# Attention slots handled two at a time: scores of two pairs in one group on TensorE, their 128x128 parts written to the transposition banks

## The chip, the cores and the metric

The kernel runs on one core of one Trainium2 chip. The metric is the device time of one execution in microseconds (us), lower is better. Engines are named as in the profile: PE is TensorE's matmul stream, PEld its weight loads, DVE VectorE, ACT ScalarE, POOL GpSimd, SP the engine that issues most of the DMAs.

## The reference, cut to what matters

```python
x = L0_attn_x                                   # (8, 256, 128)
xn = _layernorm(x)
# attention, 16 heads of 64, latent 64
q = einsum('bsd,qd->bsq', x, wq); kv = einsum('bsd,ld->bsl', x, w_kv_down)
k, v = einsum('bsl,ql->bsq', kv, w_k_up), einsum('bsl,ql->bsq', kv, w_v_up)
q, k = rope(q), rope(k)
probs = softmax(q @ k.T / sqrt(64) + causal)    # per head, 256 x 256
s = (probs @ v) @ wo.T
# eight experts of 128 -> 512 -> 128, one of them per token
g = silu(2 * expert_of_token(xn))
return x + s * g
```

## The kernel before

The attention runs over 64 pairs of heads (8 batches times 8 pairs); pair g belongs to batch g // 8. There is one slot for each pair, g = 0 to 63. The experts' part stands between slots 39 and 40 (`G_LEAD` = 40). Each engine has its own `slot(g)`, written by hand, and `program` calls it in order; the engines meet through semaphores alone, so each engine's order is exactly the order of the code.

A pair's way through the engines: PE projects q and k of two pairs in two **items** (`project(m)`, an even item is q, an odd one k), DVE multiplies them by the rotation (`rotate`, L585), POOL adds the two halves (`rotated`, L463) and SP moves them into `qk_sb` (`place`, L363). Six to eight slots later PE makes the **scores** of pair g + 2 in slot g (`scores`, L1080 the rows 128 to 255 against 256 keys, L1082 the **corner**, rows 0 to 127 against 128 keys), each for the two heads side by side in 64 rows of the array, into `s_bank[0]` and `s_bank[1]`. DVE masks them and takes the row maximum (`row_max`, L594, a corner and a rest for each head), ACT takes the exponential with the sum (`exponentials`, L885), DVE the reciprocal (`denominators`, L601), and DVE, ACT and POOL scale (`scale`: L612, L898, L474; in slots with a scatter or gather POOL scales only the 256-wide parts). PE transposes the probabilities of pair g (`turn`, L1092, three 128x128 blocks for each head, into `t_bank[0]` and `t_bank[1]`), ACT copies them to `probsT` (`turned_probs`, L907), PE multiplies with the latents (`values`, L1106 and L1108, for two pairs at once from slot 24 on), ACT copies the result (`ctx_out`, L914), and PE adds the pair's part of the batch's output into `y_bank` (`output`, L1120).

POOL also issues one indirect DMA in each of the slots 22 to 37 (`scatter`, L482: tokens sorted by expert) and 43 to 58 (`gather`, L490: the experts' results back). At the slots in `FINALS` DVE finishes a batch (`finalise`, L769 to L775) and SP stores it.

`TWICE` names the slots in which one more item is handled; before them items run 6 slots ahead, after the first 7, after the second 8. The last item, 63, falls in slot 55, so from slot 56 on there is nothing to project, rotate or stage. `ALONE` names the pairs whose values are taken singly.

The order of PE in an even slot g from 24 on: scores of g + 2, the item, `turn(g)`, an output, the values of g - 2 and g - 1. In an odd one: scores, item, turn, an output.

## Time and profile before

| what | us |
|---|---|
| median of 3 runs (310.02 to 311.63) | 310.27 |
| the profiled execution | 311.37 |
| its span, first to last instruction | 309.6 |
| PE busy | 296.1 (96%) |
| PEld busy | 237.5 (77%) |
| ACT busy | 242.8 (78%) |
| DVE busy | 221.1 (71%) |
| POOL busy | 215.8 (70%) |

The span is 1.8 us shorter than the profiled execution's own time; the median of the runs lies 1.1 us under that execution. Busy shares are averages over stages with different limits. Matmuls overlap in the records, so PE's share says little about waiting; its pace is read from the starts of successive groups. Times in the rows are from the start of the span.

### The profile page before, as it was taken

How to read it: one execution, taken by the hardware profiler on the slowest of the kernel's cores; microseconds unless marked ns; L12 is line 12 of the kernel's file. 1: busy time of each engine (PE TensorE's matmuls, PEld its weight loads, DVE VectorE, ACT ScalarE, POOL GpSimd, SP SyncE). 2: the span in 40 equal slices, each digit the busy share in tenths (PEclk: the TensorE clock that was granted, in tenths of full speed). 3: DMA queues.
4: the chain of work that ended last, by engine and by line, in shares of the span. 5: the costliest groups of instructions: out<-in, count | busy, mean ns of one | idle time of the engine just before them, and what ended most of it. 6: DMA issues, size and time to landing. Idle time of an engine off the chain costs nothing.

```text
span 309.6 us, 8479 instructions
## 1 busy us (share of the span) xinstructions
PE 296.1 (96%) x2358; PEld 237.5 (77%) x2358; DVE 221.1 (71%) x883; ACT 242.8 (78%) x851; POOL 215.8 (70%) x321
## 2 busy tenths in 40 slices
PE   8889999999999999999999989999989999899994
PEld 3578788888888888777777789999867777786763
DVE  4879998987787998988888523232268789898651
ACT  3376889898877789989897665555699999889982
POOL 3367978687777779999999943322138999889730
PEclk9987999999999999999999999999999999999998
DMA  6754595869433333333345470000063334344200
GB/s 207 231 135 112 96 263 151 216 168 298 113 69 71 65 73 86 95 87 87 88 101 138 124 210 0 2 2 0 3 186 71 89 103 112 105 109 131 74 18 18
DMA packets 39597, 33.35 MB, mean 108 GB/s; under 512 B 4802, under 2 KB 36675, under 8 KB 39555
## 3 DMA queue, kind: packets, MB, share of 16 engines
q1 hardware_dynamic: 38098, 30.51, 38.5%
q0 software_dynamic: 1024, 2.10, 2.5%
q8 instruction: 20, 0.33, 0.5%
q10 hardware_dynamic: 432, 0.23, 0.3%
q14 instruction: 23, 0.18, 0.2%
HBM read 11.07 MB, written 4.98 MB: 52 GB/s over the span
## 4 chain that ended last, share of the span: by engine, by line
PE 65%; POOL 12%; issue 11%; DVE 8%; ACT 2%; DMA 1%; POOLq 1%; SPq 0%; DVEq 0%; ACTq 0%
PE bank L1092 9%; PE bank L1080 9%; PE bank L1106 7%; PE bank L1120 6%; PE bank L1299 6%; PE bank L1284 6%; POOL probs L474 5%; POOL staged L463 4%; PE bank L1054 4%; PE bank L1082 3%; DVE rot_out L585 3%; PE bank L1108 3%; DVE masked L594 2%; PE bank L1070 2%; PE bank L1056 2%
## 5 line engine op out<-in xcount | busy, mean ns | idle before, releaser
L885 ACT ACTIVATE pexp<-masked,negmax 128x128 f32<-128x128 f32 (+1 forms) x256 | 114.1, 452 | 1.7 <-DVE negmax L594 1.6
L474 POOL TENSOR_SCALAR probs<-pexp,rden 128x256 f32<-128x256 f32 (+1 forms) x184 | 80.3, 451 | 27.0 <-DVE rden L601 24.2
L594 DVE CUSTOM_DVE_ANT_0 masked<-bank,mask 128x128 f32<-128x128 f32 (+1 forms) x256 | 75.9, 352 | 28.0 <-PE bank L1082 27.8
L463 POOL TENSOR_TENSOR staged<-rot_out 128x512 f32<-128x512 f32 x63 | 80.2, 1274 | 17.7 <-DVE rot_out L585 17.2
L585 DVE TENSOR_TENSOR rot_out<-bank,rot 128x1024 f32<-128x1024 f32 x64 | 77.7, 1215 | 4.0 <-PE bank L1056 2.7
L907 ACT COPY probsT<-bank 128x384 f32<-128x384 f32 x128 | 55.0, 480 | 23.8 <-PE bank L1092 23.2
L1092 PE MATMUL bank<-ident,probs 128*128 128x128 f32 x384 | 55.3, 278 | 1.8 <-ACT probsT L907 0.9
L885 ACT ACTIVATION_READ_ACCUMULATOR pexp<-masked,negmax 128x1 f32 x256 | 49.8, 195 | 0.0
L1080 PE MATMUL bank<-qk_sb 64*128 64x256 f32 x256 | 45.7, 434 | 2.6 <-DVE negmax L594 1.9
L1092 PEld LDWEIGHTS bank<-ident,probs 128*128 128x128 f32 x384 | 43.7, 141 | 5.0 <-POOL probs L474 1.8
L1120 PE MATMUL bank<-vo_sb,ctxT 128*128 128x128 f32 x256 | 39.5, 279 | 0.7 <-ACT ctxT L914 0.7
L1038 ACT ACTIVATE probsT<-bank,w_own 128x128 f32<-128x128 f32 x88 | 25.1, 368 | 18.8 <-PE bank L1284 18.8
L1106 PE MATMUL bank<-probsT,lat_all 128*64 128x256 f32 (+1 forms) x184 | 37.7, 488 | 0.3 <-ACT probsT L907 0.3
L1120 PEld LDWEIGHTS bank<-vo_sb,ctxT 128*128 128x128 f32 x256 | 33.7, 191 | 1.9 <-ACT ctxT L914 1.1
L549 POOL COPY w_own<-w_sb 128x516 f32 x22 | 13.5, 616 | 27.4 <-ACT probsT L1038 27.4
L1080 PEld LDWEIGHTS bank<-qk_sb 64*128 64x128 f32 x256 | 19.9, 188 | 16.2 <-issue 13.7
L1082 PEld LDWEIGHTS bank<-qk_sb 64*128 64x128 f32 x256 | 25.5, 190 | 2.7
L914 ACT COPY ctxT<-bank 128x256 f32<-128x256 f32 (+1 forms) x46 | 20.7, 451 | 6.8 <-PE bank L1108 5.6
L1082 PE MATMUL bank<-qk_sb 64*128 64x128 f32 x256 | 25.5, 275 | 0.0
L1299 PE MATMUL bank<-w_sb,probsT 128*128 x176 | 24.4, 282 | 0.7 <-issue 0.4
L1108 PEld LDWEIGHTS bank<-probsT,lat_all 128*64 128x64 f32 x184 | 13.3, 137 | 14.3 <-issue 10.3
L1284 PE MATMUL bank<-probsT,w_own 128*128 128x128 f32 x176 | 23.4, 277 | 0.7 <-DVE probsT L854 0.4
(113 smaller groups left out, 459.8 us busy)
## 6 DMA issues: line engine op xcount, KB each, us to landing
qk_sb<-staged SPq DMA_DIRECT2D x128, 128.0 KB, 2.6
w_sb<-in_w SPq DMA_DIRECT2D x2, 1024.0 KB, 5.8
w_sb<-in_w SPq DMA_DIRECT2D x4, 512.0 KB, 4.9
sorted_x<-z SPq DMA_DIRECT2D x1, 1408.0 KB, 7.9
sorted_g<-z SPq DMA_DIRECT2D x1, 1152.0 KB, 5.6
out<-res SPq DMA_DIRECT2D x8, 128.0 KB, 1.9
x_sb<-in_x SPq DMA_DIRECT2D x3, 256.0 KB, 3.2
rot<-in_c_rot SPq DMA_DIRECT2D x1, 512.0 KB, 5.6
```

The costliest lines, as they stand in the source:

```text
L463: pool.tensor_tensor(staged[:, n % 2, :, m % 2, :], rot_out[:, m % 2, :, 0:S], rot_out[:, m % 2, :, S:2 * S], op=ALU.add).then_inc(staged_ ...
L474: pool.tensor_scalar(probs[:, g % 2, i, c], pexp[:, g % 2, i, c], rden[:, g % 2, i, k:k + 1], 1.0, ALU.mult, ALU.mult).then_inc(probs_read ...
L585: dve.tensor_tensor(rot_out[:, m % 2], bank_of(m)[:].unsqueeze(1).broadcast_to([P, 2, 2 * S]), rot[:], op=ALU.mult).then_inc(rope_done, 1)
L594: t = dve.tensor_tensor_reduce(masked[:, g % 2, i, c], s_bank[i][:, c], mask[:, c], -1.0, -NEG * 1e8, ALU.add, ALU.min, negmax[:, g % 2, i ...
L885: e = act.activation(pexp[:, g % 2, i, c], masked[:, g % 2, i, c], ACT.Exp, bias=negmax[:, g % 2, i, k:k + 1], scale=-1.0, accum_out=rowsu ...
L907: act.copy(probsT[:, g % 4, i, :], t_bank[i][:, 0:SW]).then_inc(probsT_ready, 1)
L1080: pe.matmul(s_bank[i][:, P:SW], qk_sb[r, 0, p, P:S], qk_sb[r, 1, p, :], start=True, stop=True)
L1082: m = pe.matmul(s_bank[i][:, 0:P], qk_sb[r, 0, p, 0:P], qk_sb[r, 1, p, 0:P], start=True, stop=True)
L1092: t = pe.transpose(t_bank[i][:, k * P:(k + 1) * P], probs[:, g % 2, i, k * P:(k + 1) * P], ident[:])
L1106: pe.matmul(o[r, :, :], lat_all[:, 2 * b, :], probsT[:, pairs, i, 0:S], start=True, stop=False)
L1120: m = pe.matmul(y_bank[:, i * C:(i + 1) * C], ctxT[:, p, i * P:(i + 1) * P], vo_sb[:, p, :], start=(p == 0 and i == 0), stop=(p == NP - 1) ...
L1299: m = pe.matmul(bank[6 + i][:, 0:C], hidT[:, i, k, :], w2_sb[:, k, :, :].rearrange("p e c -> p (e c)")[:, bass.ds(e * C, C)], start=(k == ...
```

## The change

The slots 24 to 37 and 40 to 61 (`coupled`) are handled two at a time by a new `couple(g)` on each engine, g even. Slots 0 to 23, 38, 39, 62 and 63 keep `slot(g)`.

- PE: `scores_of_two(g + 2)` makes the rests of two pairs into the two halves of `s_bank`, then the two pairs' corners into columns 0 to 255 of `t_bank`. The corners wait until ACT has copied the transposes of pair g - 1 out of that bank. Then come both items, `turn(g)`, the outputs of g - 4 and g - 3, `turn(g + 1)`, and the values of g - 2 and g - 1. `turn` waits for a new semaphore, `corner_read`: DVE must have read both corners.
- DVE: `row_max` becomes `corner_max` (both pairs' corners at once, at the couple's start) and `rest_max`; around them the denominators, scales, rotations and finals of the two slots.
- ACT: within a couple the copies of turned probabilities, the exponentials of pairs g + 2 and g + 3 and, last, `ctx_out(g - 2)`; it used to stand between the two halves of an exponential.
- POOL and SP: the old order of the two slots. `TWICE` goes from (36, 38) to (23, 38), so items run 7 ahead from slot 24 instead of 36.
- Outputs come a couple later; slots 38 and 62 hold one more `output` each, of pairs 34 and 58.

```diff
...
-TWICE = (36, 38)
+TWICE = (23, 38)
...
+def coupled(g):
+    return FIRST_DOUBLE <= g < G_LEAD - 2 or G_LEAD <= g < B * NP - 2
+def corners_through(g):
+    return sum(1 for n in range(g + 1) if coupled(n - 2))
...
-        def program(start, slot, finish, experts):
+        def program(start, slot, couple, finish, experts):
...
-                slot(g)
+                if not coupled(g):
+                    slot(g)
+                elif g % 2 == 0:
+                    couple(g)
...
-                if g + 1 < B * NP and g != G_LEAD:
+                if g + 1 < B * NP:
...
+            def couple(g):
+                for n in range(g, g + 2):
+                    if n != G_LEAD:
+                        scale(n + 1)
+                    for m in items(n):
+                        rotated(m)
+                    if SCATTER_SLOT <= n < SCATTER_SLOT + NT:
+                        scatter(n - SCATTER_SLOT)
+                    if GATHER_SLOT <= n < GATHER_SLOT + NT:
+                        gather(GATHER_ORDER[n - GATHER_SLOT])
...
+            def corner_max(g):
+                dve.wait_ge(scores_done, g + 1)
+                wait(dve, exp_done, 2 * g - 2)
+                for i in range(2):
+                    t = dve.tensor_tensor_reduce(masked[:, g % 2, i, 0:P], t_bank[i][:, g % 2 * P:(g % 2 + 1) * P], mask[:, 0:P],
+                                                 -1.0, -NEG * 1e8, ALU.add, ALU.min, negmax[:, g % 2, i, 0:1])
+                t.then_inc(corner_read, 1)
+            def rest_max(g):
+                for i in range(2):
+                    dve.tensor_tensor_reduce(masked[:, g % 2, i, P:SW], s_bank[i][:, g % 2 * S:(g % 2 + 1) * S], mask[:, P:SW],
+                                             -1.0, -NEG * 1e8, ALU.add, ALU.min,
+                                             negmax[:, g % 2, i, 1:2]).then_inc(masked_ready, 1)
...
-                if 0 < g // NP < LEAD and g % NP == (2 if NP * (g // NP) <= FIRST_DOUBLE else 3):
+                if 0 < g // NP < LEAD and g % NP == (2 if NP * (g // NP) < FIRST_DOUBLE else 3):
...
-                if g + 1 < B * NP and g != G_LEAD:
+                if g + 1 < B * NP:
...
+            def couple(g):
+                corner_max(g + 2)
+                corner_max(g + 3)
+                if g != G_LEAD:
+                    denominators(g + 1)
+                    scale(g + 1)
+                rest_max(g + 2)
+                for m in items(g):
+                    rotate(m)
+                if (g + 1) // NP < LEAD and (g + 1) % NP == 3:
+                    take_y((g + 1) // NP - 1)
+                if FINALS.get(g + 1, -1) >= LEAD:
+                    finalise(FINALS[g + 1])
+                rest_max(g + 3)
+                denominators(g + 2)
+                scale(g + 2)
+                for n in range(g, g + 2):
+                    if FINALS.get(n, LEAD) < LEAD:
+                        finalise(FINALS[n])
+                for m in items(g + 1):
+                    rotate(m)
...
-                more = g + 1 < B * NP and g != G_LEAD
+                more = g + 1 < B * NP and not coupled(g - 1)
...
-                if g > 1 and g - 2 in ALONE and g not in (G_LEAD, G_LEAD + 1):
+                if g > 1 and g - 2 in ALONE:
...
-                if g % 2 and g > 2 and g - 3 not in ALONE and g not in (G_LEAD + 1, B * NP - 1):
+                if g % 2 and g > 2 and g - 3 not in ALONE and g != B * NP - 1:
...
-                if more:
+                if g + 1 < B * NP:
...
+            def couple(g):
+                if g == FIRST_DOUBLE:
+                    exponentials(g + 1, 0)
+                    ctx_out(g - 2)
+                    exponentials(g + 1, 1)
+                if g != G_LEAD:
+                    scale(g + 1)
+                turned_probs(g)
+                for i in range(2):
+                    exponentials(g + 2, i)
+                turned_probs(g + 1)
+                scale(g + 2)
+                for i in range(2):
+                    exponentials(g + 3, i)
+                if g == FIRST_DOUBLE:
+                    ctx_out(g - 1)
+                elif g != G_LEAD:
+                    ctx_out(g - 2)
...
+            def scores_of_two(g):
+                pe.wait_ge(masked_ready, 2 * g)
+                for n in range(2):
+                    p = (g + n) % NP
+                    pe.wait_ge(qk_in[p], 32 * (g // NP) + 32)
+                    for i, r in enumerate(half_rows):
+                        pe.matmul(s_bank[i][:, n * S:(n + 1) * S], qk_sb[r, 0, p, P:S], qk_sb[r, 1, p, :], start=True, stop=True)
+                pe.wait_ge(probsT_ready, 2 * (g - 2))
+                for n in range(2):
+                    p = (g + n) % NP
+                    for i, r in enumerate(half_rows):
+                        m = pe.matmul(t_bank[i][:, n * P:(n + 1) * P], qk_sb[r, 0, p, 0:P], qk_sb[r, 1, p, 0:P],
+                                      start=True, stop=True)
+                m.then_inc(scores_done, 2)
...
+                wait(pe, corner_read, corners_through(g + 3 - g % 2))
...
-                if g > 2 and g - 3 not in ALONE and g not in (G_LEAD, G_LEAD + 1, G_LEAD + 2):
+                if g in (G_LEAD - 2, B * NP - 2):
+                    output(g - 4)
+                if g > 2 and g - 3 not in ALONE:
...
-                if g > 1 and g - 2 in ALONE and g not in (G_LEAD, G_LEAD + 1):
+                if g > 1 and g - 2 in ALONE:
...
-                if g > 0 and g - 1 in ALONE and g != G_LEAD:
+                if g > 0 and g - 1 in ALONE:
...
-                if g > 1 and g % 2 == 0 and g - 2 not in ALONE and g != G_LEAD:
+                if g > 1 and g % 2 == 0 and g - 2 not in ALONE:
...
+            def couple(g):
+                scores_of_two(g + 2)
+                for m in (*items(g), *items(g + 1)):
+                    project(m)
+                turn(g)
+                if g == FIRST_DOUBLE:
+                    output(g - 2)
+                elif g == FIRST_DOUBLE + 2:
+                    output(g - 3)
+                elif g not in (G_LEAD, G_LEAD + 2):
+                    output(g - 4)
+                    output(g - 3)
+                turn(g + 1)
+                if g == FIRST_DOUBLE:
+                    values(g - 1)
+                elif g != G_LEAD:
+                    values(g - 2)
...
```

Left out are the line that makes `corner_read`, the calls that pass `couple`, and SP's `couple`, which calls `slot` twice.

PE in the second half, from the output ahead of the scores of pair 54 to the first matmul of the next item, in the kernel before (bank0 and bank1 are `s_bank`, bank2 and bank3 `t_bank`, bank7 `y_bank`, bank6 the values'):

```order
L1120 MATMUL bank7<-vo_sb,ctxT 128x128 [waits ctx_ready,y_read]
L1120 MATMUL bank7<-vo_sb,ctxT 128x128
L1080 MATMUL bank0<-qk_sb 128x256 [waits masked_ready,qk_in6]
L1080 MATMUL bank1<-qk_sb 128x256
L1082 MATMUL bank0<-qk_sb 128x128
L1082 MATMUL bank1<-qk_sb 128x128
L1054 MATMUL bank4<-xnT_h,wq_h 128x256 [waits rope_done]
L1055 MATMUL bank4<-xnT_l,wq_h 128x256
L1056 MATMUL bank4<-xnT_h,wq_l 128x256
L1054 MATMUL bank4<-xnT_h,wq_h 128x256
```

The same place in the changed kernel, here for pairs 62 and 63, the last group, from the values ahead of it to the transposes of pair 60:

```order
L1209 MATMUL bank6<-probsT,lat_all 64x512 [waits probsT_ready,ctx_ready]
L1209 MATMUL bank6<-probsT,lat_all 64x512
L1211 MATMUL bank6<-probsT,lat_all 64x2x128 x2
L1178 MATMUL bank0<-qk_sb 128x256 [waits qk_in6,masked_ready]
L1178 MATMUL bank1<-qk_sb 128x256
L1178 MATMUL bank0<-qk_sb 128x256 [waits qk_in7]
L1178 MATMUL bank1<-qk_sb 128x256
L1183 MATMUL bank2<-qk_sb 128x128 [waits probsT_ready]
L1183 MATMUL bank3<-qk_sb 128x128
L1183 MATMUL bank2<-qk_sb 128x128
L1183 MATMUL bank3<-qk_sb 128x128
L1195 MATMUL bank2<-ident,probs 128x128 [waits probs_ready00,probsT_ready,corner_read]
```

Two pairs' scores stand together, their corners in bank2 and bank3 and behind a wait for `probsT_ready`; the first transpose waits for `corner_read` too. In couples 24 to 54 two items stand between the corners and that transpose, in 56, 58 and 60 nothing.

PE in slot 62 before, from the outputs of pairs 58 (slot 61) and 59 to the first transpose of pair 62:

```order
L1120 MATMUL bank7<-vo_sb,ctxT 128x128 [waits ctx_ready]
L1120 MATMUL bank7<-vo_sb,ctxT 128x128
L1120 MATMUL bank7<-vo_sb,ctxT 128x128 [waits ctx_ready]
L1120 MATMUL bank7<-vo_sb,ctxT 128x128
L1106 MATMUL bank6<-probsT,lat_all 64x512 [waits probsT_ready,ctx_ready]
L1106 MATMUL bank6<-probsT,lat_all 64x512
L1108 MATMUL bank6<-probsT,lat_all 64x2x128 x2
L1092 MATMUL bank2<-ident,probs 128x128 [waits probs_ready00,probsT_ready]
```

and in the changed kernel, from the values of pairs 58 and 59, the end of couple 60, to the first transpose of pair 62:

```order
L1209 MATMUL bank6<-probsT,lat_all 64x512 [waits probsT_ready,ctx_ready]
L1209 MATMUL bank6<-probsT,lat_all 64x512
L1211 MATMUL bank6<-probsT,lat_all 64x2x128 x2
L1223 MATMUL bank7<-vo_sb,ctxT 128x128 [waits ctx_ready]
L1223 MATMUL bank7<-vo_sb,ctxT 128x128
L1223 MATMUL bank7<-vo_sb,ctxT 128x128 [waits ctx_ready]
L1223 MATMUL bank7<-vo_sb,ctxT 128x128
L1209 MATMUL bank6<-probsT,lat_all 64x512 [waits probsT_ready,ctx_ready]
L1209 MATMUL bank6<-probsT,lat_all 64x512
L1211 MATMUL bank6<-probsT,lat_all 64x2x128 x2
L1195 MATMUL bank2<-ident,probs 128x128 [waits probs_ready00,probsT_ready,corner_read]
```

Before, the values of 58 and 59 stood a slot further ahead of output 58, with scores and a turn between; now they stand directly before it.

ACT at the same place before, from the exponentials of pair 62 to the copy of the values of pairs 60 and 61 (L914 the second time):

```order
L885 ACTIVATE pexp,rowsum<-masked,negmax 128x128 [waits probs_ready00,masked_ready]
L885 ACTIVATE pexp,rowsum<-masked,negmax 128x256 [waits probs_ready01]
L914 COPY ctxT<-bank6 128x512 [waits y_step,pv_done]
L885 ACTIVATE pexp,rowsum<-masked,negmax 128x128 [waits probs_ready10,masked_ready]
L885 ACTIVATE pexp,rowsum<-masked,negmax 128x256 [waits probs_ready11]
L907 COPY probsT<-bank2 128x384 [waits probsT_done,pv_done]
L907 COPY probsT<-bank3 128x384 [waits probsT_done]
L885 ACTIVATE pexp,rowsum<-masked,negmax 128x128 [waits probs_ready00,masked_ready]
L885 ACTIVATE pexp,rowsum<-masked,negmax 128x256 [waits probs_ready01]
L885 ACTIVATE pexp,rowsum<-masked,negmax 128x128 [waits probs_ready10,masked_ready]
L885 ACTIVATE pexp,rowsum<-masked,negmax 128x256 [waits probs_ready11]
L914 COPY ctxT<-bank6 128x512 [waits y_step,pv_done]
```

and in the changed kernel, again from the exponentials of pair 62 on:

```order
L952 ACTIVATE pexp,rowsum<-masked,negmax 128x128 [waits probs_ready00,masked_ready]
L952 ACTIVATE pexp,rowsum<-masked,negmax 128x256 [waits probs_ready01]
L952 ACTIVATE pexp,rowsum<-masked,negmax 128x128 [waits probs_ready10,masked_ready]
L952 ACTIVATE pexp,rowsum<-masked,negmax 128x256 [waits probs_ready11]
L974 COPY probsT<-bank2 128x384 [waits probsT_done,pv_done]
L974 COPY probsT<-bank3 128x384 [waits probsT_done]
L952 ACTIVATE pexp,rowsum<-masked,negmax 128x128 [waits probs_ready00,masked_ready]
L952 ACTIVATE pexp,rowsum<-masked,negmax 128x256 [waits probs_ready01]
L952 ACTIVATE pexp,rowsum<-masked,negmax 128x128 [waits probs_ready10,masked_ready]
L952 ACTIVATE pexp,rowsum<-masked,negmax 128x256 [waits probs_ready11]
L981 COPY ctxT<-bank6 128x512 [waits y_step,pv_done] x2
```

The copy of the values of pairs 58 and 59 stood in the middle of the exponentials of pair 62; now it is the first of the two copies in the last row, behind the exponentials of 62 and 63 and the copy of turned pair 61.

## Rows read from the trace of the kernel before

**Rows 1.** Busy time by stretch: window, length, then each engine's busy us (xcount), clock.
```profile
115.67:176.81 61.14, 60.62 (x474) 46.85 (x474) 50.19 (x180) 52.58 (x193) 57.95 (x73) 1.00 0.37 95
223.79:239.55 15.76, 14.67 (x113) 11.50 (x112) 11.67 (x51) 15.39 (x48) 9.29 (x15) 1.00 0.47 126
239.55:282.90 43.35, 41.94 (x325) 32.06 (x325) 38.33 (x142) 39.23 (x142) 39.40 (x49) 1.00 0.40 105
```

**Rows 2.** Timeline of POOL, one slot with a scatter: start, us, engine, line, operation, xcount.
```profile
138.56 1.27 POOL L463 TENSOR_TENSOR staged<-rot_out 128x512 f32<-128x512 f32 x1
140.00 1.06 POOL L482 DMA_INDIRECT sorted_x<-xn,pos  x1 [0.17 <-issue]
141.11 0.93 POOL L474 TENSOR_SCALAR probs<-pexp,rden 128x256 f32<-128x256 f32 x2
```

**Rows 3.** Timeline of PE over two slots, 136.63 to 143.57.
```profile
136.63 0.70 PE L1080 MATMUL bank<-qk_sb 64*128 64x256 f32 x4
137.17 0.39 PE L1082 MATMUL bank<-qk_sb 64*128 64x128 f32 x4
137.48 0.39 PE L1054 MATMUL bank<-xnT_h,wq_h 128*128 128x256 f32 x1
...
138.30 0.82 PE L1092 MATMUL bank<-ident,probs 128*128 128x128 f32 x6
138.96 0.61 PE L1120 MATMUL bank<-vo_sb,ctxT 128*128 128x128 f32 x4
139.50 1.08 PE L1106 MATMUL bank<-probsT,lat_all 128*64 128x512 f32 x4
...
140.94 0.70 PE L1080 MATMUL bank<-qk_sb 64*128 64x256 f32 x4
...
143.57 0.49 PE L1080 MATMUL bank<-qk_sb 64*128 64x256 f32 x2
```

**Rows 4.** POOL's waits from 239.55 to 282.90 (total, times, longest), and two gathers.
```profile
POOL staged L463 <- DVE rot_out L585: 1.2, 3, 0.4
...
243.03 1.05 POOL L490 DMA_INDIRECT xn<-sorted_g,pos  x1 [0.16 <-issue]
...
282.90 1.18 POOL L490 DMA_INDIRECT xn<-sorted_g,pos  x1 [0.17 <-issue]
```

**Rows 5.** Timeline of DVE in one slot; a DVE scale beside a POOL addition; another scale.
```profile
138.19 0.29 DVE L594 CUSTOM_DVE_ANT_0 masked<-bank,mask 128x128 f32<-128x128 f32 x1
138.40 0.42 DVE L594 CUSTOM_DVE_ANT_0 masked<-bank,mask 128x256 f32<-128x256 f32 x1
...
139.85 1.21 DVE L585 TENSOR_TENSOR rot_out<-bank,rot 128x1024 f32<-128x1024 f32 x1
...
131.98 1.04 DVE L612 TENSOR_SCALAR probs<-pexp,rden 128x128 f32<-128x128 f32 x1
...
131.67 1.26 POOL L463 TENSOR_TENSOR staged<-rot_out 128x512 f32<-128x512 f32 x1
...
257.33 0.29 DVE L612 TENSOR_SCALAR probs<-pexp,rden 128x128 f32<-128x128 f32 x1
```

**Rows 6.** Timeline of ACT near the end: copy, start of an exponential, next copy.
```profile
297.52 0.86 ACT L907 COPY probsT<-bank 128x384 f32<-128x384 f32 x2
298.26 0.41 ACT L885 ACTIVATE pexp<-masked,negmax 128x128 f32<-128x128 f32 x1
...
300.13 0.59 ACT L914 COPY ctxT<-bank 128x512 f32<-128x512 f32 x1
```

**Rows 7.** Timeline of PE without items: scores of 58 and 62; outputs; `turn(62)`.
```profile
279.30 0.70 PE L1080 MATMUL bank<-qk_sb 64*128 64x256 f32 x4
...
291.99 0.70 PE L1080 MATMUL bank<-qk_sb 64*128 64x256 f32 x4
...
297.59 1.06 PE L1120 MATMUL bank<-vo_sb,ctxT 128*128 128x128 f32 x8
...
300.02 0.88 PE L1092 MATMUL bank<-ident,probs 128*128 128x128 f32 x6
```

14 lines of the change are left out of this document (9 added, 5 removed).

## The prediction, made before the changed kernel was run

> **What bounds the kernel now.** I read the busy shares first, then busy time by stretch, then the timeline of each engine in one slot. The page's shares name PE (96%), but matmul records overlap, and in the slots that the change touches a second engine is as full. From 115.67 to 176.81, slots 22 to 39, POOL is busy for 57.95 of 61.14 us [rows 1]; the rest is mostly gaps like the 0.17 ahead of its scatter [rows 2]. One slot of POOL is an addition (from 138.56), a scatter (140.00) and two scales (141.11, 0.9): **3.45 us** [rows 2]. PE's two slots from 136.63 to 143.57 take 6.94, 3.47 a slot, with no wait in them [rows 3]. So PE and POOL run at one pace, and a faster PE meets POOL 0.02 us a slot later. From 239.55 to 282.90 POOL has the gathers in place of the scatters: twelve gathers apart, its mean is 3.61 a slot where its own work is about 3.45 (39.40 us busy, and it waits 1.2 us for DVE's rotations alone [rows 1, 4]). Between the experts and that stretch ACT is the full one, 15.39 of 15.76 us [rows 1]. In slots 56 to 63 nothing is projected, and short chains between all four engines decide.
>
> **What the change removes on PE.** Each scores group is made in 64-row halves, everything around it in 128 rows. Four records of `output` are busy for 0.61 us and eight for 1.06, so four more cost 0.45; from four to a group of the other form it is 0.54 (138.96 to 139.50), 0.09 more [rows 3, 7]. Six transposes take 0.66 (138.30 to 138.96), 0.11 for each record of 128 columns; two heads side by side should need 0.22 for the corners and 0.44 for the rests, and take 0.31 and 0.54: 0.09 and 0.10 more [rows 3]. The first record behind the group I take to lose the same. Together 0.40 us for one isolated group. One group instead of two: **PE gains 0.40 us a couple**, bounds 0.20 (two switches) and 0.42, so a couple with items would take 6.94 - 0.40 = 6.54. There are 18 couples, 7.2 us at most.
>
> **Where that gain meets a bound.** Seven couples (24 to 36) lie beside the scatters. POOL's order keeps all its work, 6.90 us a couple, and the experts cannot start before POOL's last additions and weight copies. Moving `TWICE` to 23 moves one addition of 1.27 us from slot 36 to slot 23, within the stretch in which POOL is full: no change in the sum, but in couple 24 the second turn waits for POOL's scale of pair 25, one addition later. Gain there: 0.
>
> **What it adds there: a loop.** I lay one couple out from the rows, t = 0 at its first scores. PE: scores to 1.5 (2 x 0.85 - 0.20), last corner landed 1.6. DVE: four corners at 0.21, to 2.45; denominators, scale, two rests at 0.35, to 3.65; rotation 1.21, to 4.9 [rows 5]. Only then can POOL add; before, the rotation came after one pair's maxima, now after one and a half. From that addition it is one POOL round (6.90) to the scale that the second turn of the next couple waits for, then 0.4 of turn, 1.5 of values and switch, and 4.9 again: 13.7 for two couples, 6.85 each. That ties with POOL's 6.90. But a DVE scale that meets a POOL addition ends with it: 1.04 us from 131.98, where the addition runs from 131.67 to 132.93; the one at 257.33, beside no addition, takes 0.29 [rows 5]. With the couple's layout the first scale falls into the addition of the slot before (from about 1.5 to 2.8), so I add 0.1 us a couple: **7.0**. Bounds 6.85 and 7.4 (a whole scale of 1.04 in every couple, half of it on the loop). For slots 24 to 39 that is 7 x 0.1, less what slots 38 and 39 absorb: **+0.5 us**, range -0.2 to +1.5.
>
> The Trainium skill, GPSIMD Engine Reference, section Key points, says that GpSimd shares its SBUF interfaces with VectorE and that VectorE's instructions with two SBUF inputs or in a two-port mode contend. The row of 1.04 agrees. By that rule alone, with every scale of a couple on DVE held, the couple would come out at the upper bound, 7.4, and the time near 320.
>
> **Slots 40 to 55.** Entry: DVE's corners of pair 45 now stand ahead of the denominators of 43, and wait for ACT's exponentials of 43, while ACT is full. Laid out from 223.79, the gather of slot 44 comes at about 244.4, against 243.03 [rows 4]: +1.3. From there to slot 55 before took 282.90 - 243.03 = 39.87 for eleven slots [rows 4]; at 3.5 a slot it is 38.5, and about 0.5 comes back for the finals, whose 0.85 us on DVE now also delay the corners. Net **+0.4**, range -2.0 to +2.0; the lower end is all of POOL's idle time there gone.
>
> **Slots 56 to 63.** No items cover the corners. PE's scores end at 1.5 and `turn` starts at 2.6, when `corner_read` is there: PE idle for 1.1. The couple is 2.6 + 0.65 turn + 0.88 outputs + 0.65 turn + 1.54 values = 6.3. Before, the four slots from scores 58 to scores 62 took 12.7 [rows 7]; two couples take 12.7 to 12.9. So far nothing. Then the end. Before, from scores 62 at 291.99 to `turn(62)` at 300.02: 8.0 us [rows 7]. Now scores of 62 and 63 at t = 0, `turn(60)` ends at 3.25, outputs 4.1, `turn(61)` 4.8, values of 58 and 59 6.3. Slot 62 opens with output 58, which waits for ACT's copy of these values. ACT comes to it last: copy of turned 60 from 3.1, 0.74; exponentials of 62, 1.87; copy of 61, 0.74; exponentials of 63, 1.87; then the copy, 0.59 [rows 6]: 8.9. PE then has outputs 58 and 59 (0.98) and the values of 60 and 61 (1.44), so `turn(62)` comes at 11.3 instead of 8.0: **+3.3 us**, range +1.5 (half the stall if ACT finds the exponentials early) to +4.5. Behind `turn(62)` the two kernels have the same steps (309.6 - 300.0 = 9.6).
>
> **The sum.** 0.5 + 0.4 + 3.3 = +4.2. Against the profiled execution that is a span of 309.6 + 4.2 = 313.8 and, with its 1.8 around the span, 315.6; the median of the runs lies 1.1 lower, so **314.5 us**.
>
> **The rivals.**
> - *PE was the bound* (faster). For it: PE's records leave no gap, and PE holds most of the chain that ended last. If all of POOL's idle time beside the gathers vanishes (12 x 0.16 = 2) and the end costs nothing, 308.3; if POOL could follow everywhere, -7.2, 303.1. It decides where POOL's rounds stay under PE's 6.54, and they are 6.90. Chance 0.14.
> - *It cancels* (within 0.5%, 1.55 us, about what a measurement of this kernel can tell from no change). Half the stall at the end (+1.6) and -1.5 beside the gathers: about 310.5. Chance 0.16.
> - *The scores keep their switches*: two groups cost as before, since corners and rests alternate banks and the second pair waits for its `qk_sb`. Then PE's couple is 6.94 plus what it waits for, 7.1: 15 x 0.1 more than my sum, 316. Chance 0.08.
> - *DVE against POOL* (clearly slower). Each couple locks in at 7.4, because POOL's addition holds DVE's scale, this delays the rotation, and so the next addition: 15 x 0.4 = 6 more, 320. For it: the 1.04 us scale. Against: the scale of 0.29, with POOL at its gather, and the fact that before ran at 3.45 with such holds in it. Chance 0.12.
>
> **How the numbers follow.** My forecast (312 to 317) has 0.50. Slower by over 0.5% is 0.50 + 0.08 + 0.12 = 0.70, no difference 0.16, faster 0.14. For 8 in 10 the range leaves out the larger gains (0.10) below and the full lock-in (0.08) above: 309.0 to 318.5.
>
> **What would show it.** Right: POOL's scatters stay 3.45 to 3.5 apart and PE shows waits for POOL's `probs` at the second turn; in couples 56 to 60 PE idles about 1.1 us before the first turn, released by DVE; after the values of 58 and 59 PE idles 2 to 2.5 us, released by ACT's `ctxT`; scores groups take about 1.5 us for two pairs. Wrong: gathers less than 3.4 apart, `turn(62)` less than 9 us after scores 62, or a couple of 6.5 with POOL idle. If the couples beside the scatters take 7.3 or more, the fourth rival holds.

## The result, and the profile after

The changed kernel takes **318.14 us** (median of 4 runs, 317.82 to 318.83) where the kernel before, on the same chip, takes 310.95 (310.02 to 312.36): a ratio of 1.0227, 95% interval 1.0198 to 1.0256. The profiled execution took 318.06 with a span of 316.3, 6.7 longer than the 309.6 of before. The range held it; the point was 3.6 us too low. Of all executions that follow, one of `a_nodma_mask` (315.3 us, 1.5% above the fastest of that kernel) counts as slow, and its ratio leaves it out.

First the page of the changed kernel: span, and busy us of each engine with its share.

```profile
span 316.3 us, 8461 instructions
...
PE 293.8 (93%) x2358; PEld 233.4 (74%) x2358; DVE 218.1 (69%) x883; ACT 242.1 (77%) x851; POOL 216.4 (68%) x321
```

PE's share fell from 96% to 93%: PE has less to do and waits more. Busy time by stretch of the changed kernel: window, length, busy us of PE, PEld, DVE, ACT, POOL, granted clock, DMA share, GB/s. The first three answer to [rows 1] (the third begins at the gather of slot 44 and ends at that of slot 55); the last two are the couples without items and the end.

```profile
115.64:177.16 61.52, 59.82 (x472) 45.18 (x471) 47.35 (x179) 51.50 (x190) 58.06 (x73) 1.00 0.38 97
224.44:241.58 17.14, 13.91 (x111) 10.56 (x110) 11.07 (x48) 15.10 (x46) 9.35 (x15) 1.00 0.45 116
245.51:284.89 39.38, 37.14 (x292) 27.66 (x291) 34.63 (x131) 34.73 (x127) 35.90 (x44) 1.00 0.37 100
281.81:295.25 13.44, 11.09 (x91) 7.91 (x89) 9.09 (x45) 11.84 (x45) 10.53 (x15) 1.00 0.34 88
295.25:316.30 21.05, 13.51 (x106) 9.73 (x104) 6.41 (x29) 10.99 (x38) 4.60 (x10) 1.00 0.06 18
```

Beside the scatters PE is busy for 0.8 us less than before and the stretch is 0.4 longer. PE over one couple with a scatter (compare [rows 3]), and POOL beside it ([rows 2]):

```profile
145.11 1.13 PE L1178 MATMUL bank<-qk_sb 64*128 64x256 f32 x8
146.08 0.61 PE L1183 MATMUL bank<-qk_sb 64*128 64x128 f32 x8
146.62 0.39 PE L1156 MATMUL bank<-latT,wk_h 128*128 128x256 f32 x1
...
147.91 0.82 PE L1195 MATMUL bank<-ident,probs 128*128 128x128 f32 x6
148.56 1.06 PE L1223 MATMUL bank<-vo_sb,ctxT 128*128 128x128 f32 x8
149.46 1.19 PE L1195 MATMUL bank<-ident,probs 128*128 128x128 f32 x6
150.58 1.08 PE L1209 MATMUL bank<-probsT,lat_all 128*64 128x512 f32 x4
...
152.02 0.49 PE L1178 MATMUL bank<-qk_sb 64*128 64x256 f32 x2
```

```profile
144.65 1.06 POOL L500 DMA_INDIRECT sorted_x<-xn,pos  x1 [0.17 <-issue]
...
148.12 1.06 POOL L500 DMA_INDIRECT sorted_x<-xn,pos  x1 [0.17 <-issue]
149.22 0.93 POOL L492 TENSOR_SCALAR probs<-pexp,rden 128x256 f32<-128x256 f32 x2
150.13 1.27 POOL L481 TENSOR_TENSOR staged<-rot_out 128x512 f32<-128x512 f32 x1
```

The scores of two pairs take 1.51 us. Both turns are six records, but the first lasts 0.65 (147.91 to 148.56) and the second 1.12 (149.46 to 150.58), since it stops for POOL's scales of 149.22 (PEld records 0.27 of waiting for POOL's `probs` at 149.76, and where nothing holds the second turn it lasts 0.75, see a_nodma_mask). Scatters stand 3.47 apart, the couple lasts 6.91, and before two slots lasted 6.94.

The entry behind the experts, on ACT (first two lines, and the last) and DVE (third line):

```profile
228.70 1.28 ACT L952 ACT_TABLE_LOAD   x1
231.76 0.83 ACT L974 COPY probsT<-bank 128x384 f32<-128x384 f32 x2
...
234.50 0.29 DVE L632 CUSTOM_DVE_ANT_0 masked<-bank,mask 128x128 f32<-128x128 f32 x1 [0.58 <-ACT pexp L952]
...
235.70 0.86 ACT L974 COPY probsT<-bank 128x384 f32<-128x384 f32 x2 [1.35 <-PE bank L1195]
```

The longest wait of PE from 224 to 239.2 (total, times, longest):

```profile
PE bank L1183 <- ACT probsT L974: 1.9, 1, 1.9
```

PE's corners of pairs 44 and 45 (L1183) go into the transposition banks, where the turned pair 41 still lies; ACT copies it out at 231.76, behind the table load and the exponentials of 42. PE stands for 1.9 us.

The end, PE from the scores of 62 on, and ACT's copy for which it stops ([rows 6, 7]):

```profile
295.25 1.14 PE L1178 MATMUL bank<-qk_sb 64*128 64x256 f32 x8
...
297.91 0.87 PE L1195 MATMUL bank<-ident,probs 128*128 128x128 f32 x6 [1.09 <-DVE negmax L632]
...
301.06 0.84 ACT L974 COPY probsT<-bank 128x384 f32<-128x384 f32 x2
301.79 0.41 ACT L952 ACTIVATE pexp<-masked,negmax 128x128 f32<-128x128 f32 x1
...
303.56 0.57 ACT L981 COPY ctxT<-bank 128x512 f32<-128x512 f32 x1
...
304.18 1.16 PE L1223 MATMUL bank<-vo_sb,ctxT 128*128 128x128 f32 x8 [2.41 <-ACT ctxT L981]
...
306.71 0.33 PE L1195 MATMUL bank<-ident,probs 128*128 128x128 f32 x1
```

`turn(62)` comes 11.46 us after the scores of 62 (306.71 - 295.25); before it was 8.03.

**Where the 6.7 us are.** The table cuts each profiled execution at the starts of PE's scores of pairs 21, 41, 42, 46, 58, 62 and the end of the span. 21 to 41 holds the coupled slots with scatters, 41 to 42 the experts, 42 to 46 the entry, 46 to 58 the gathers, 58 to 62 the couples without items. A star marks a stretch in which PE's granted clock fell below 0.93; such a stretch is not to be compared (more on this at the end). The kernels are told in the next section.

| kernel | 21-41 | 41-42 | 42-46 | 46-58 | 58-62 | 62-end |
|---|---|---|---|---|---|---|
| before | 71.80 | 53.16 | 13.08 | 42.43 | 12.69 | 17.61 |
| after | 72.90 | 52.75 | 14.25 | 43.12 | 13.44 | 21.05 |
| a_ctx | 72.94 | 52.58 | 15.06* | 43.27 | 13.44 | 19.33 |
| a_end | 72.87 | 52.88 | 14.25 | 43.09 | 12.77 | 17.61 |
| a_entry | 72.90 | 52.57 | 13.08 | 42.96 | 13.44 | 22.53* |
| a_both | 72.88 | 52.83 | 13.07 | 43.45 | 12.77 | 17.66 |
| b_nodma | 70.98 | 53.29 | 14.67* | 41.59 | 11.73 | 17.85 |
| a_nodma | 71.77 | 53.09 | 15.03* | 41.98 | 13.77 | 22.41* |
| a_nodma_mask | 69.60 | 52.88 | 14.75* | 40.77 | 13.14 | 22.58* |
| a_mask | 72.86 | 52.60 | 14.08 | 42.91 | 13.37 | 21.09 |
| a_both_off | 71.89 | 53.11 | 13.08 | 44.35 | 12.76 | 17.76 |
| a_best | 71.72 | 52.78 | 14.66* | 43.92 | 12.77 | 17.64 |
| b_off | 70.93 | 53.17 | 13.08 | 42.66 | 12.75 | 17.62 |
| b_twice | 71.97 | 53.23 | 13.08 | 42.45 | 12.68 | 17.58 |

After against before: +1.10, -0.41, +1.17, +0.69, +0.75, +3.44, together 6.7. No stretch with couples is shorter than before. What lies ahead of the scores of pair 21 isn't in the table: every kernel here does the same work there, and it takes 97.2 to 99.1 us from one execution to the next (98.83 before, 98.79 after). Spans and medians of two kernels can differ by as much without any part in the change, so the stretches say more.

### The profile page after: what moved, and what is told of

It reads as the page before. It is cut to its first block and busy times, and to the rows that moved or that the text cites. A ratio compares the mean times of both kernels' runs of the same rounds, so it can differ in the third digit from the quotient of the medians.

```text
span 316.3 us, 8461 instructions
## 1 busy us (share of the span) xinstructions
PE 293.8 (93%) x2358; PEld 233.4 (74%) x2358; DVE 218.1 (69%) x883; ACT 242.1 (77%) x851; POOL 216.4 (68%) x321
## 5 line engine op out<-in xcount | busy, mean ns | idle before, releaser
L1195 PE MATMUL bank<-ident,probs 128*128 128x128 f32 x384 | 58.3, 281 | 7.1 <-DVE negmax L632 3.7
L623 DVE CUSTOM_DVE_ANT_0 masked<-bank,mask 128x128 f32<-128x128 f32 x112 | 33.2, 352 | 11.8 <-PE bank L1168 11.7
L1223 PE MATMUL bank<-vo_sb,ctxT 128*128 128x128 f32 x256 | 37.2, 279 | 3.2 <-ACT ctxT L981 3.1
L1223 PEld LDWEIGHTS bank<-vo_sb,ctxT 128*128 128x128 f32 x256 | 32.5, 191 | 5.1 <-ACT ctxT L981 4.4
L639 DVE CUSTOM_DVE_ANT_0 masked<-bank,mask 128x256 f32<-128x256 f32 x72 | 27.1, 415 | 0.0
L632 DVE CUSTOM_DVE_ANT_0 masked<-bank,mask 128x128 f32<-128x128 f32 x72 | 17.1, 287 | 13.4 <-PE bank L1183 11.4
L1422 PEld LDWEIGHTS bank<-w_sb,probsT 128*128 128x128 f32 x176 | 21.3, 191 | 3.5 <-issue 3.5
L1140 PE MATMUL bank<-xnT_h,wq_h 128*128 128x256 f32 x64 | 20.8, 325 | 1.7 <-DVE rot_out L614 1.4
```

The lines of the kernel that those rows point to most:

```text
L623: t = dve.tensor_tensor_reduce(masked[:, g % 2, i, c], s_bank[i][:, c], mask[:, c], -1.0, -NEG * 1e8, ALU.add, ALU.min, negmax[:, g % 2, i ...
L639: dve.tensor_tensor_reduce(masked[:, g % 2, i, P:SW], s_bank[i][:, g % 2 * S:(g % 2 + 1) * S], mask[:, P:SW], -1.0, -NEG * 1e8, ALU.add, A ...
L1195: t = pe.transpose(t_bank[i][:, k * P:(k + 1) * P], probs[:, g % 2, i, k * P:(k + 1) * P], ident[:])
L1223: m = pe.matmul(y_bank[:, i * C:(i + 1) * C], ctxT[:, p, i * P:(i + 1) * P], vo_sb[:, p, :], start=(p == 0 and i == 0), stop=(p == NP - 1) ...
L1422: m = pe.matmul(bank[6 + i][:, 0:C], hidT[:, i, k, :], w2_sb[:, k, :, :].rearrange("p e c -> p (e c)")[:, bass.ds(e * C, C)], start=(k == ...
```

## The experiments

My theory: beside the scatters and gathers POOL keeps the couples at its own pace, and the loss comes from the end (ACT's copy in the wrong place), the entry (ACT full) and the uncovered corners. The rivals: every couple loses alike; TensorE was the bound; the scores keep their switches; DVE against POOL. The first four kernels undo a piece of the change each.

**The copy at the end alone (a_ctx).**

```diff
                 turned_probs(g + 1)
                 scale(g + 2)
+                if g == B * NP - 4:
+                    ctx_out(g - 2)
                 for i in range(2):
                     exponentials(g + 3, i)
...
-                elif g != G_LEAD:
+                elif g not in (G_LEAD, B * NP - 4):
                     ctx_out(g - 2)
```

> The changed kernel with one step of ScalarE's order moved: in the last couple (slots 60, 61) the copy of the values of pair 58 stands between the copy of the turned pair 61 and the exponentials of pair 63, no longer behind these. If the wait of 2.41 us ahead of output 58 (304.18) is what lengthened the end, the copy comes 1.9 us earlier: 2.0 us less than the changed kernel (bounds 1.0, if the exponentials of pair 63, now later, hold up the end instead, and 2.4), so about 316 us. If the end is longer because of the couples' own chain, or if TensorE was the bound, it stays at 318.

Measured: 317.09 us (316.26 to 317.71), ratio to before 1.0177 (1.0106 to 1.0247), 1.05 less than the changed kernel. The last stretch fell from 21.05 to 19.33. Its ACT and PE:

```profile
302.44 0.59 ACT L981 COPY ctxT<-bank 128x512 f32<-128x512 f32 x1
...
303.08 1.16 PE L1225 MATMUL bank<-vo_sb,ctxT 128*128 128x128 f32 x8 [0.69 <-ACT ctxT L981]
```

The stall of 2.41 is 0.69, and the stretch gives back exactly that difference, 1.72: the place of this copy is half of the end's loss. The other half goes with the last couples (next kernel); I take it to be their shape, scores of two pairs and then 1.1 us without work until the corners are read. The median gained less than the stretch, near the lower bound. In the profiled execution 0.8 of the gain is lost again in the starred stretch at the entry, where the program is unchanged.

**No couples in the last eight slots (a_end).**

```diff
-    return FIRST_DOUBLE <= g < G_LEAD - 2 or G_LEAD <= g < B * NP - 2
+    return FIRST_DOUBLE <= g < G_LEAD - 2 or G_LEAD <= g < B * NP - NP
...
-                if g in (G_LEAD - 2, B * NP - 2):
+                if g in (G_LEAD - 2, B * NP - NP):
                     output(g - 4)
```

> The changed kernel with couples up to slot 55 only; slots 56 to 63 go one by one as in the kernel before. My theory puts 3.4 us of the loss behind the scores of pair 62 and 0.75 us into the two couples without items (56 and 58): 4.2 us less than the changed kernel, about 314. A loss that every couple causes alike (DVE against POOL, or the scores keeping their switches; 18 couples for 6.7 us, 0.37 each) would give back four couples, 1.5 us: 316.6.

Measured: **314.11 us** (10 runs, 312.47 to 315.31), ratio 1.0087 (1.0054 to 1.0119), 4.0 less. The stretches 58 to 62 and 62 to the end are those of before to 0.1 us, all others as in the changed kernel. The last two (the window of the second ends 0.1 short of the span):

```profile
280.32:293.09 12.77, 12.37 (x94) 8.84 (x93) 9.03 (x45) 12.00 (x46) 10.39 (x14) 1.00 0.37 101
293.09:310.60 17.51, 13.52 (x100) 9.44 (x100) 6.37 (x29) 10.64 (x37) 4.70 (x10) 0.95 0.06 16
```

"Every couple loses alike" would have left it at 316.6. More than half of the whole loss lies in the last eight slots.

**No couples in slots 40 to 43 (a_entry).** Beside `coupled`, the steps at the seams follow (which slot takes over outputs, values, exponentials); they add nothing.

```diff
-    return FIRST_DOUBLE <= g < G_LEAD - 2 or G_LEAD <= g < B * NP - 2
+    return FIRST_DOUBLE <= g < G_LEAD - 2 or G_LEAD + 4 <= g < B * NP - 2
```

> The changed kernel with slots 40 to 43 one by one and couples from slot 44. If what was lost behind the experts (1.8 us between the scores of pair 42 and the gather of slot 44) is the corners that wait for a ScalarE that is full, it goes, except for what the same corners cost at the new entry: 1.2 to 1.8 us less than the changed kernel, about 316.7. If the entry costs the same wherever it stands (a cost of changing the order, not of the full ScalarE), or if every couple loses alike (two couples, 0.7), 317.4 to 318.

Measured: 317.22 us (316.0 to 318.66), ratio 1.0175 (1.0096 to 1.0254), 0.9 less; by the median alone it lies between both. The stretches tell more: 42 to 46 is 13.08, exactly that of before, and 46 to 58 is 0.16 shorter, so 1.33 is gained, within my bounds. The same entry of couples, four slots later, shows no cost there. The span shows none of it, because PE's clock fell in the last stretch of this execution:

```profile
293.77:316.20 22.43, 15.01 (x106) 10.33 (x104) 6.40 (x29) 11.05 (x38) 4.60 (x10) 0.88 0.06 17
```

**Both edits (a_both).** The two diffs together.

> Couples from slot 24 to 37 and 44 to 55 only, the edits of the two kernels before together. Mine: the losses add, 4.2 + 1.5 = 5.7 less than the changed kernel, 312.4 and 1.5 above the kernel before; what is left is the couples beside a full POOL, which gain nothing. If TensorE was the bound there, 13 couples at -0.4 would bring it to about 306. If every couple loses 0.37, 13 couples leave it 4.8 above the kernel before, 315.8.

Measured: **312.73 us** (10 runs, 311.51 to 313.51), ratio 1.0041 (1.0007 to 1.0074), 5.4 less than the changed kernel against a forecast of 5.7. The losses add, and "TensorE was the bound" (306) falls. Thirteen couples are left, beside a POOL with scatters or gathers, and they gain nothing. By the stretches they lose: 21 to 41 takes 72.88 against 71.80, and 46 to 58 43.45 against 42.43, 1.0 to 1.1 each. The first of the two, here and (below) in the kernel before:

```profile
98.04:170.92 72.88, 71.20 (x573) 54.90 (x571) 58.77 (x232) 62.38 (x231) 64.59 (x86) 1.00 0.39 92
```

```profile
98.83:170.63 71.80, 71.49 (x572) 56.29 (x570) 61.31 (x232) 62.84 (x232) 63.50 (x83) 1.00 0.38 93
```

**Is it POOL that keeps the gain?** Both kernels without POOL's indirect DMAs. This leaves out the moving of the tokens to their experts and back (all sixteen scatters, of the slots 22 to 37, and all sixteen gathers); SP waits for the zeroed rows instead of the scatters.

```diff
-                pool.indirect_dma_start(
-                    out=sorted_x, out_offset=bass.IndirectOffsetOnAxis(ap=pos[:, n:n + 1], axis=0),
-                    in_=xn[:, n, :], in_offset=None).then_inc(scattered, 16)
...
-                pool.wait_ge(scattered, 16 * NT)
                 pool.wait_ge(g_out, 32)
-                pool.indirect_dma_start(
-                    out=gate[:, n, :], out_offset=None, in_=sorted_g,
-                    in_offset=bass.IndirectOffsetOnAxis(ap=pos[:, n:n + 1], axis=0)).then_inc(g_in[n // 2], 16)
...
-                dve.wait_ge(g_in[b], 32)
```

> The kernel before without POOL's indirect DMAs (the scatters of slots 24 to 39 and the gathers) and the waits for them; the tokens are not moved, so the experts work on zeros and the outputs are not the reference's. It shows what TensorE does in single slots when POOL has about 2.3 us of work for each (3.45 less some 1.1 for the DMA's descriptors). Mine, by which TensorE and POOL run at one pace: two slots beside the experts' forerun go from 6.94 to 6.8 to 6.94, and the span shrinks by under 3 us. If POOL was the slower of the two, two slots fall well below 6.8.

Measured (b_nodma): 307.78 us (307.03 to 309.51), ratio 0.9884 (0.9845 to 0.9922). Two slots still take 6.92 (scores at 132.45, 139.37, 146.30): TensorE's own time, with POOL at two thirds. TensorE and POOL did run at one pace, as the prediction had it.

> The changed kernel with the same parts left out (POOL's indirect DMAs and the waits for them; outputs not the reference's). With POOL relieved the couples show TensorE's own gain: mine, 6.55 a couple (6.4 to 6.7) where the same cut of the kernel before has 6.9, so the changed order gains about 0.35 a couple that POOL keeps from it otherwise, and the time of this kernel against that cut is about 1 above to 2 below. If the scores keep their switches, a couple stays at 6.9 and this kernel stays 6 us or more above that cut. If DVE's loop is the limit, 6.85.

Measured (a_nodma): 317.34 us (316.15 to 318.80), ratio 1.0186 (1.0137 to 1.0235). Couples go at **6.75** (scores at 144.26, 151.01, 157.76, and at 245.92, 252.67, 259.42), neither the 6.55 of my theory nor the 6.85 of DVE's loop, with POOL busy for 4.60 of them. My expectation for the whole time left out the entry and the end, and was wrong by more than 8 us for that; the couples are what the run was for. TensorE's own work in a couple is 1.51 scores, 1.30 items, 0.65 + 0.65 turns, 0.89 outputs, 1.44 values: 6.45. (The second turn is put too low there: ahead of the values it lasts 0.75 even where nothing holds it, so the work is 6.54.) So a second bound stood behind POOL's. DVE and PE in one such couple:

```profile
146.65 0.29 DVE L626 CUSTOM_DVE_ANT_0 masked<-bank,mask 128x128 f32<-128x128 f32 x1 [0.25 <-ACT pexp L945]
...
146.95 0.28 PE L1135 MATMUL bank<-xnT_h,wq_l 128*128 128x256 f32 x1
147.22 0.87 PE L1188 MATMUL bank<-ident,probs 128*128 128x128 f32 x6
```

The items end at 147.07 (0.12 after their last start), and `turn` starts at 147.22. It must not overwrite the corners before DVE has read them; DVE must not overwrite `masked` before ACT has made the exponentials of the pair two before; ACT makes those after its copies of what the last `turn` left. That is a ring through three engines that the change closes by putting the corners into the transposition banks.

**The ring cut open (a_nodma_mask, a_mask).** One corner in eight (head 1 of every fourth pair) gets a buffer of its own. DVE waits for one head's exponentials less before an odd pair's corners.

```diff
-        negmax = sb("negmax", [P, 2, 2, 2])
+        negmax = sb("negmax", [P, 4, 2, 2])
+        spare = sb("spare", [P, P])
+
+        def masked_part(g, i, k):
+            if g % 4 == 3 and i == 1 and k == 0:
+                return spare[:]
+            return masked[:, g % 2, i, rows[k]]
...
             def corner_max(g):
...
-                wait(dve, exp_done, 2 * g - 2)
+                wait(dve, exp_done, 2 * g - 2 - g % 2)
...
             def rest_max(g):
 
+                wait(dve, exp_done, 2 * g - 2)
```

> The changed kernel without POOL's indirect DMAs and the waits for them (the tokens are not moved, so the outputs are not the reference's), and with a buffer of its own for the masked corner of head 1 of every fourth pair, so that VectorE's corner of a couple's second pair need not wait for ScalarE's last exponentials of the pair two before. In the same cut without that buffer the couples took 6.75 us where TensorE's records add up to 6.45, and the first turn started 0.15 behind the items. If the loop (ScalarE's exponentials, VectorE's corner, TensorE's turn, ScalarE's copy) makes the 6.75, couples go to 6.5 to 6.6 and the time from 317.3 to 314.5 (13 couples at 0.2). If it is something else (TensorE's own work, VectorE's rotations), 6.75 and 317 stay.

Measured (a_nodma_mask): **312.49 us** (10 runs, 310.58 to 315.3), ratio 1.0021 (0.9983 to 1.0059), 4.85 less than without the buffer; of the 5.6 between the two profiled spans, 1.3 lies ahead of the scores of 21 and has nothing to do with it. Couples go at 6.53 to 6.54 (scores at 141.47, 148.01, 154.54). DVE no longer waits at the corners of the second pair (the first line is head 0; the second is head 1, in the new buffer), and `turn` follows the items at once:

```profile
143.53 0.28 DVE L632 CUSTOM_DVE_ANT_0 masked<-bank,mask 128x128 f32<-128x128 f32 x1
143.74 0.28 DVE L632 CUSTOM_DVE_ANT_0 spare<-bank,mask 128x128 f32<-128x128 f32 x1
...
144.15 0.28 PE L1142 MATMUL bank<-xnT_h,wq_l 128*128 128x256 f32 x1
144.27 0.82 PE L1195 MATMUL bank<-ident,probs 128*128 128x128 f32 x6
```

The ring was the second bound. With both bounds gone the coupled order is the faster one where it has items: 21 to 41 in 69.60 against 70.98 of b_nodma, 46 to 58 in 40.77 against 41.59. The gain is bigger than I forecast (3.4 us in these two stretches alone), since the first couples after each entry were held longer than 6.75 (7.39, 7.08 and 7.08).

> The changed kernel with that buffer alone. Mine: beside the full POOL nothing moves (couples stay at 6.91), the entry behind the experts gains up to 0.6 (the corner of pair 45 waits for one head's exponentials less): 317.3 to 318.1. If the corner's wait is what limits the couples in the whole kernel, 13 couples at 0.2 to 0.3 and the entry: 314 to 315.

Measured (a_mask): 317.92 us (316.72 to 318.9), ratio 1.0192 (1.0124 to 1.0261), no different from the changed kernel. In the whole kernel the same buffer gives nothing: POOL's bound comes first. It also corrects the entry: the wait of DVE's corner (0.58, at 234.50) is gone, 42 to 46 is only 0.17 shorter, and PE's wait is still there:

```profile
PE bank L1190 <- ACT probsT L981: 1.9, 1, 1.9
```

**POOL relieved with its DMAs kept (b_off, a_both_off, a_best).** POOL's 256-wide scale of head 0 of even pairs goes to DVE, 0.46 us of POOL in two slots.

```diff
+            if busy and k and i == 0 and g % 2 == 0 and coupled(g - 1):
+                return "vector"
             return "pool" if k or not busy else ("vector", "scalar")[i]
```

(in b_off with `FIRST_DOUBLE < g` for `coupled(g - 1)`; a_both_off is a_both with this edit, a_best is a_both_off with the buffer.)

> The kernel before with the same scale of every even pair moved from POOL to DVE, from slot 26 on. Mine: TensorE's 3.47 a slot is the bound as soon as POOL is relieved, so at most the 1.2 to 2 us of POOL's excess beside the gathers: 309 to 311. If POOL alone sets the slots' pace, 16 pairs at 0.46, up to 5 less: 306.

Measured (b_off): 310.65 us (309.44 to 311.75), ratio 0.9986 (0.9962 to 1.0010). No change that can be measured; two slots take 6.93. TensorE is the bound once POOL is relieved.

> Couples 24 to 37 and 44 to 55, and POOL's 256-wide scale of head 0 of the even pair of each couple made by DVE, so POOL has 0.46 us less in a couple. Mine: couples fall from 6.9 to about 6.5 (POOL 6.44, TensorE 6.54) in the thirteen couples, 3 to 4.5 us less than the same kernel without that edit, about 308. If DVE's loop with a held scale is the limit, nothing or a loss of up to 3, since DVE gets 0.3 to 1.0 us more in it.

Measured (a_both_off): 313.3 us (311.73 to 314.05), ratio 1.0059 (1.0035 to 1.0082); a_both has 312.73. A miss by 5 us. Beside the scatters it does what it should: couples of 6.53 to 6.87, and 21 to 41 falls by 1.0. Beside the gathers it loses 0.9 again (44.35 against 43.45). Half of that, 0.47, is the couple in which DVE also adds up two finished tiles: 8.79 from 258.03, against 8.32 in a_both, with 0.56 us in which PE waits for DVE's rotation (at 261.07). That DVE's added scales do the rest too is likely and not shown.

> Couples 24 to 37 and 44 to 55 only, POOL's 256-wide scale of head 0 of the even pairs made by VectorE, and the buffer for the masked corners: both loops relieved (POOL 6.44 a couple, TensorE 6.45). Mine: couples at 6.5 to 6.6 instead of 6.75, 2 to 3 us less than the 313.3 without the buffer, so 310.5 to 311.5, level with the kernel before; the couples in which VectorE adds up a finished tile keep their 0.5 to 1.0. If VectorE is the limit once it has the scales, it stays at 313.

Measured (a_best): 312.72 us (10 runs, 311.69 to 314.27), ratio 1.0025 (0.9997 to 1.0052). The interval touches that of a_both_off, so the 0.6 between them isn't shown; a gain of 2 to 3 is ruled out. Couples alternate between 6.53 and 6.87. In a long one the second turn is held, for 0.33 more than in a short one, by a scale that POOL starts only after its next scatter (at 141.59):

```profile
141.87 1.15 PE L1207 MATMUL bank<-ident,probs 128*128 128x128 f32 x6
142.95 1.08 PE L1221 MATMUL bank<-probsT,lat_all 128*64 128x512 f32 x4
```

**The other part of the change alone (b_twice).**

```diff
-TWICE = (36, 38)
+TWICE = (23, 38)
```

> The kernel before with the step of two projections in one slot moved from slot 36 to slot 23 alone (this part of the change by itself). Mine: no change, within 0.3 us of the kernel before, since POOL's work from slot 22 to 39 keeps its sum. If the earlier addition pushes POOL's first scatters, or the freed slot 36 lets the experts start earlier, plus or minus 1.3 (one addition).

Measured: 311.38 us (10 runs), ratio 0.9996 (0.9961 to 1.0030). No change, as said. None of the kernels that do the whole work is faster than the kernel before by more than its interval.

## Why the prediction was right, and where it wasn't

**POOL keeps the gain: right, and shown from both sides.** PE's gain was there (the scores of two pairs take 1.51, forecast 1.5; the couple without its bounds takes 6.53, forecast 6.54). The Trainium skill, TensorEngine Tiling (Array Packing), section Key Properties, says that changing the tiling mode drains the TensorE. The runs agree in that each change costs time: one group of 64-row records instead of two saves 0.20 us in the scores and 0.4 in the couple, from 6.92 (b_nodma) to 6.53 (a_nodma_mask).

**"0.1 us a couple" beside the scatters: wrong reason, small term.** I forecast couples of 7.0, +0.1 for a DVE scale held by POOL's addition. They took 6.91. The hold is real and falls elsewhere. In the kernel before, 19 scales of 128x128 begin inside a POOL addition; the twelve that have 0.24 us or more of it ahead of them end 0.08 to 0.10 us behind its end (0.34 to 1.04 us long), the seven with 0.20 or less take 0.28 or 0.29. So the scale at 139.17 ends with the addition from 138.56 [rows 2]. In the changed kernel ten scales in a row, from 133.98 to 165.17, begin in the last 0.17 us of an addition and take 0.29, such as the one at 147.79 (addition 146.67 to 147.96); eight others in that kernel are held, for about 0.2 us at most. My layout had the right addition and the wrong part of it. With this the rival of 7.4 a couple fell: not because nothing is held, but because the couple's order moves the scale to where the hold costs nothing. First the kernel before, then (last line) the changed one:

```profile
139.17 0.76 DVE L612 TENSOR_SCALAR probs<-pexp,rden 128x128 f32<-128x128 f32 x1
...
262.07 2.12 DVE L775 TENSOR_TENSOR res<-gated,x_sb 128x256 f32<-128x256 f32 x1
262.64 1.27 POOL L463 TENSOR_TENSOR staged<-rot_out 128x512 f32<-128x512 f32 x1
...
283.19 0.42 DVE L775 TENSOR_TENSOR res<-gated,x_sb 128x256 f32<-128x256 f32 x1
...
147.79 0.29 DVE L657 TENSOR_SCALAR probs<-pexp,rden 128x128 f32<-128x128 f32 x1
```

DVE's sum of a finished tile (`res`) is held as well: 0.42 us away from POOL's additions, 2.12 across one, and in the changed kernel 1.42 (at 265.36, the addition runs from 265.23 to 266.49); both end 0.3 behind the addition. The Trainium skill, GPSIMD Engine Reference, section Key points, names VectorE's instructions with two SBUF inputs among those that contend with GpSimd; these rows, with the two inputs `gated` and `x_sb`, agree.

The stretch lost 0.65 up to the scores of 42 (forecast 0.5): 1.10 between the scores of 21 and of 41, less 0.41 in the experts' stretch (why that one is shorter is open) and 0.04 by which it began earlier. The 1.10 isn't spread over the couples. From the scores of 28 to those of 30 it is 7.53, against 6.64 before, with 0.73 of PE waiting for POOL's `probs` (at 129.04); from 40 to 41, where slot 38 makes one more output, it is 5.84 against 5.37. The item that `TWICE` moves adds 0.90 between the scores of 25 and 26 and takes 0.91 away between those of 38 and 40. So the size came out near for a reason that I didn't have: luck.

**The second bound: missed.** I looked at one loop for PE's couple (POOL, DVE, 6.85) and didn't see the ring through ACT, `masked` and the transposition banks. It cost nothing here because POOL stood before it. But the case for "PE was the bound" would have failed on it as well: relieving POOL alone brings 6.75, not 6.54.

**The entry: right place, wrong wait.** Forecast +1.3 at the gather of slot 44 (from a layout that the prediction doesn't show), measured +1.83 (2.48 less the 0.65 there already). I had DVE's corner of pair 45 wait for ACT's exponentials of 43. That wait exists (0.58), but without it only 0.17 comes back (a_mask). The 1.9 us are PE's: its corners need the banks in which the turned pair 41 lies until ACT, full, has copied it. The sentence that ACT is full was right, the resource was the wrong one. a_entry returns the 1.17 in that stretch.

**Gathers: -0.49 instead of -0.87.** 39.38 for eleven slots, forecast 39.0. The term for DVE's finished tiles was a little small: the couple with one of them took 7.82 (259.70 to 267.52), as long as before (7.78). In both, `res` is held by POOL's addition (above), and PE then waits for DVE's row maxima, 0.33 now and 0.78 before.

**Couples without items: the term that failed.** I put the two couples at 12.7 to 12.9 and "so far nothing". Between the scores of 58 and of 62 it was +0.75 (13.44 against 12.69). Another +0.52 had no term at all: the sum goes from POOL's gather of slot 55 over to PE's scores of 58, and these come 3.08 us ahead of that gather now, 3.60 before. Part of what POOL gained over the gathers PE never had. Together it is 1.27 from the gather of slot 55 to the scores of 62 (10.36 against 9.09). PE's idle time before the first turn was as forecast, 1.03 and 1.10, released by DVE. But the couple of 6.3 that I summed takes 6.96 and 6.48: in the first one the second turn stops once more, for POOL's `probs`, since slots 56 to 59 still have gathers:

```profile
284.43 0.88 PE L1195 MATMUL bank<-ident,probs 128*128 128x128 f32 x6 [1.03 <-DVE negmax L632]
...
286.52 0.89 PE L1195 MATMUL bank<-ident,probs 128*128 128x128 f32 x5 [0.21 <-POOL probs L492]
```

The before side hides such a stop too: its 12.69 holds 0.62 of waiting for POOL (at 281.11). Without POOL's DMAs those four slots take 11.73 in singles and 13.77 in couples, so the couples without cover cost 2.0, not nothing; 0.6 of this is the ring again (13.14 with the buffer, a_nodma_mask). a_end gives 0.67 back here.

**The end: right, by its mechanism and its size.** Forecast +3.3 with `turn(62)` at 11.3 us, measured +3.43 and 11.46; ACT's copy forecast at 8.9 behind the scores ended at 8.9 (304.13). a_ctx ties 1.7 of it to that copy's place, a_end all of it to the last couples.

The sum: 0.65 + 1.83 - 0.49 + 0.52 + 0.75 + 3.43 = 6.7, where I had 0.5 + 1.3 - 0.9 + nothing + 0.0 + 3.3 = 4.2. Every term was too low. The miss of 2.5 is made of the couples without items (0.75), the entry (0.53), the step from POOL's gather to PE's scores (0.52), the gathers (0.38), and 0.28 in the other two.

## What to carry to other kernels

Before grouping work to save an engine's time, find what ends each of its rounds; where two engines run at one pace, the saving is worth nothing until both are relieved, and the edges of the grouping (where its cover of other work is missing) are then all that shows in the time. When a buffer takes on a second use, draw the ring anew: who must have read it, what that reader waits for, and whether this leads back to the writer; a ring can lie hidden behind another bound and appears only once that is lifted. An in-order engine should make what the next group of the bound engine needs first ahead of long work that nobody waits for yet.
